# Reordering the start of each expert: preparation pieces between the additions and the reciprocal, the root ahead of the square, the first keys and queries behind the last variance

## The reference, cut to what matters

```python
def _expert(x, p):
    h = _ln(jax.nn.relu(x @ ew1 + eb1) @ ew2 + eb2, eg, ebeta)   # 128 -> 256 -> 256, layer norm: "the encoder"
    qkv = h @ aiw + aib
    q, k, v = jnp.split(qkv, 3, axis=-1)                         # 16 heads of 16
    attn = jax.nn.softmax(jnp.einsum('bhqd,bhkd->bhqk', q, k) * SCALE, axis=-1)
    ...                                                          # out projection, two LSTMs, gates, decoder
```

## Time and profile before

| | us |
|---|---|
| median of 3 runs | 4192.47 |
| lowest, highest | 4190.81, 4195.63 |
| the profiled execution | 4191.02 |
| its span in the trace | 4189.3 |

### The profile page before, as it was taken

How to read it: one execution, slowest core, us unless ns; L and a number is a source line. 1 busy time by engine, 2 the same in 40 slices (tenths; PEclk the granted TensorE clock), 3 DMA queues, 4 the chain that set the end, 5 groups by cost and what they waited for, 6 DMA issues and landing times. The chain is left out here.

```text
span 4189.3 us, 98294 instructions
## 1 busy us (share of the span) xinstructions
PE 3695.9 (88%) x36068; PEld 2265.2 (54%) x36068; DVE 2841.8 (68%) x5015; ACT 2150.3 (51%) x4378; POOL 1278.5 (31%) x1076
## 2 busy tenths in 40 slices
PE   5869689979988998952999999999999959999998
PEld 4645346646655655631555555555555527666665
DVE  8966568858858857876666666666666664555555
ACT  4536437737746755755444444444444445555554
POOL 0027537627726736744000000000000003444443
PEclk8889899989999999975999999999999978999999
DMA  8910100010010011025111111111111131111111
GB/s 174 176 33 0 52 18 2 1 56 2 0 42 16 0 42 32 0 87 157 46 50 48 45 48 50 48 44 48 49 49 43 49 103 52 54 53 53 53 53 30
DMA packets 392895, 205.07 MB, mean 49 GB/s; under 512 B 151221, under 2 KB 386474, under 8 KB 392106
## 3 DMA queue, kind: packets, MB, share of 16 engines
q1 hardware_dynamic: 392354, 203.09, 18.9%
q10 hardware_dynamic: 392, 0.03, 0.0%
HBM read 145.55 MB, written 57.51 MB: 48 GB/s over the span
## 5 line engine op out<-in xcount | busy, mean ns | idle before, releaser
L1827 PE MATMUL banks<-l_w,l_xs 128*64 128x512 f16 x6240 | 722.3, 381 | 15.0 <-DVE l_xs L1875 14.2
L1827 PE MATMUL banks<-l_w,l_hs 128*64 128x512 f16 x6144 | 705.8, 379 | 1.7 <-DVE l_hs L1881 1.7
L1827 PEld LDWEIGHTS banks<-l_w,l_xs 128*64 128x64 f16 x6240 | 344.6, 110 | 330.7 <-issue 25.6
L1827 PEld LDWEIGHTS banks<-l_w,l_hs 128*64 128x64 f16 x6144 | 348.3, 110 | 316.7 <-DVE l_hs L1881 2.2
L194 POOL MEMSET h_ident<- 128x128 f32 x1 | 0.2, 204 | 1444.3 <-POOLq L81 1444.3
L985 POOL TENSOR_TENSOR ax_p<-ax_p,ax_ri 128x520 f32<-128x520 f32 (+1 forms) x256 | 320.0, 1251 | 267.4 <-DVE ax_ri L1185 267.4
L1932 DVE SCALAR_TENSOR_TENSOR l_gates<-banks,l_unscale,l_bias 128x1024 f32<-128x1024 f32 x260 | 333.8, 1284 | 96.1 <-PE banks L1827 94.7
L1988 ACT ACTIVATE l_gates<-l_gates 128x768 f32<-128x768 f32 x260 | 219.1, 843 | 347.4 <-DVE l_gates L1932 347.4
L2259 PE MATMUL banks<-h_mem,h_w 128*128 128x320 f16 x2496 | 357.9, 300 | 1.0 <-DMA h_mem<-mem_scratch 1.0
L2554 ACT ACTIVATE h_work<-banks,h_bias,h_factor 128x320 f32<-128x320 f32 x312 | 192.3, 616 | 262.8 <-PE banks L2259 259.1
L2259 PEld LDWEIGHTS banks<-h_mem,h_w 128*128 128x128 f16 x2496 | 244.4, 98 | 94.9 <-issue 1.6
(11 more groups left out here) (306 smaller groups left out, 7180.4 us busy)
## 6 DMA issues: line engine op xcount, KB each, us to landing
image<-in_x_dram SPq DMA_DIRECT2D x192, 196.0 KB
l_x<-x_scratch SPq DMA_DIRECT2D x130, 256.0 KB, 3.0
mem_scratch<-l_hs SPq DMA_DIRECT2D x520, 64.0 KB, 1.9
h_mem<-mem_scratch SPq DMA_DIRECT2D x104, 320.0 KB, 3.7
x_scratch<-x_out SPq DMA_DIRECT2D x4, 4160.0 KB, 16.4
raw_in<-in_L_ffn_attn_in_w_dram SPq DMA_DIRECT2D x4, 768.0 KB, 4.5
h_scratch<-x_out SPq DMA_DIRECT2D x1, 2080.0 KB, 6.5
z_scratch<-z SPq DMA_DIRECT2D x1, 2080.0 KB, 11.6
```

Source lines behind the costliest of these rows:

```text
L1827: mm = pe.matmul(ps[d * HALF:(d + 1) * HALF, 2 * z + n, :], lhsT, w_of[e][:, d, kk, b, n * 512:(n + 1) * 512], start=(kk == 0 and turn_ == ...
```

## The change

It reorders instructions within the encoder and the hand-over of each expert; no arithmetic is added or taken away.

- DVE: the pieces stand between additions and reciprocal, and the first four of them one step later (2 to 5, not 1 to 4). `begin_second` stands behind the last reciprocal.
- ACT: the root stands ahead of the square. The first unit's keys are kept at step 11 and not behind the class queries and values.
- PE: the products with beta stand behind step 1 (a function of their own) and not behind step 0; values, turn and share of the largest magnitude one step later; keys and queries of the first unit behind the last variance (step 11). In unit 0, PE waits for the kept class values before the next unit's keys go into the bank that they are read from.
- POOL: the first keys are masked ahead of the class queries, and before the wait for these.

```diff
@@ pool_run
+        mask_keys(base, 0, 0, base * GROUP)
         pool.wait_ge(self.first_kept, BASE + 2 * e + 1)
         mask_class(0, base * GROUP)
-        mask_keys(base, 0, 0, base * GROUP)
@@ pe_run, unit_
                 if s == 1 and self.unit_in(u, 1):
+                    if u == 0:
+                        pe.wait_ge(self.first_kept, BASE + 2 * e + 2)
@@ act_run
         act.wait_ge(self.first_kept, BASE + 2 * e + 2)
-        self.act_keys(act, ps[:, 6, :], factor, base, 0)
@@ experts_stage, tensor
+                def sum_betas():
+
                     at = VECTORS["beta"][0]
...
-                laid_steps(body, {0: sum_vectors, 2: sum_values, 3: turn_most, 4: share_most, WSTEPS: begin})
+                laid_steps(body, {0: sum_vectors, 1: sum_betas, 3: sum_values, 4: turn_most, 5: share_most, WSTEPS + 1: begin})
@@ experts_stage, vector
-                between = {1: gain_weights, 2: measure, 3: reduce_most, 4: size, 6: lambda: low_half(0),
+                between = {2: gain_weights, 3: measure, 4: reduce_most, 5: size, 6: lambda: low_half(0),
                            7: lambda: low_half(1).then_inc(w_low, 1), 8: begin_first,
-                           9: lambda: att.dve_split(dve, e * att.UNITS, 0, e * att.UNITS * GROUP), WSTEPS: begin_second}
+                           9: lambda: att.dve_split(dve, e * att.UNITS, 0, e * att.UNITS * GROUP)}
...
                                               ALU.add).then_inc(h2_kept, 1)
+                    if k in between:
+                        between[k]()
                     if live(2):
                         dve.wait_ge(rooted, BASE + at - 1)
...
-                laid_steps(body, between)
+                laid_steps(body, {})
+                begin_second()
@@ experts_stage, scalar
+                    if live(2):
+                        act.wait_ge(varied, BASE + at_ - 1)
...
+                        act.activation(sd[:, par, :], ps[:, 4, 0:WIDE], ACT.Sqrt, bias=eps[:, 0:1]).then_inc(rooted, 1)
                     if live(1):
...
                         act.activation(sq[:, 1 - par], hc[:, (slot - 1) % RING], ACT.Square).then_inc(squared, 1)
-                    if live(2):
...
-                laid_steps(body, {5: raise_weights})
+                laid_steps(body, {5: raise_weights, WSTEPS + 1: lambda: att.act_keys(act, ps[:, 6, :], factor[:, 0:1], e * att.UNITS, 0)})
```

More of the change, by code:

```diff
@@ L1645, in body @@
                                            bias=vec[:, at + m:at + m + 1]).then_inc(h1_kept, 1)
+                    if live(2):
+                        act.wait_ge(varied, BASE + at_ - 1)
+                        if live(4):
+                            act.wait_ge(inverted, BASE + at_ - 3)
+                        act.activation(sd[:, par, :], ps[:, 4, 0:WIDE], ACT.Sqrt, bias=eps[:, 0:1]).then_inc(rooted, 1)
                     if live(1):
```

## The result

The changed kernel takes 4163.38 us (median of 4 runs, 4160.95 to 4168.73), the kernel before on the same chip 4191.67 (4 runs, 4190.81 to 4195.63): ratio 0.9932, 95% interval 0.9915 to 0.995, 28.3 us less. The forecast was 4156, its range 4147 to 4174. In a later comparison the same two gave 4163.66 and 4191.3, ratio 0.9932 [0.9919, 0.9946]. The profiled execution took 4165.48 us, 25.5 less than that of before.

What follows compares the result with a forecast made beforehand. It took PE at mostly 1.2 GHz to bound the lead-in and a DVE, ACT, DVE loop the later steps. Gains of 3.8 + 31.4 + 1.6 = 36.8 us off 4191.02 gave 4154.2, as median 4156; range 4147 to 4174.

Steps and rivals of the forecast that it cites:

- Bound and loop: Encoder's later steps: the loop DVE, ACT, DVE sets 6.17 us a step; root first breaks it, leaving PE's 5.59.
- Steady steps: Encoder, step 2 to step 9: PE sets the pace, 40.5 us against 41.45 before; square, relu and `measure` hidden.
- Tail: Encoder's end, behind step 9: step 2 to POOL's last product takes 59.0 us, was 66.85; stretch wins 31.4 in all.
- Keys and queries' move: First unit's, to behind the last variance: little by itself; up to 3 us an expert returns if their cover went.
- Lead-in: Encoder steps 0 and 1: clock rises at 7.9 us, work ends at 12.7 against 14.4; 3.8 us won in all.
- the drop behind the single columns: Lead-in: single-column products at full clock may let the clock drop again; even chance, priced 0.9 us an expert.
- Hand-over: Encoder to attention: earlier key masking gains 1.1 to 1.2 us, delays class split 0.7; net 0.4, 1.6 in all.
- rival 2: Hand-over: class split waits for the whole first key masking; gain 0.1, not 0.4 us an expert; 4157 us; chance 0.10.
- The failed step: Behind each encoder: everything waits for its last `h`, so time won there moves the rest forward whole, losing none.
- Rivals 1, 3 and 4: DVE stays the pace, 4177 us (0.15); attention or LSTM waits for a load, 4192 (0.04); ACT's queue slows steps, 4225 (0.03).
- rival 1: Encoder steps: DVE stays the pace near 6 us, POOL's product reaching into the pieces' gap; 4177 us; chance 0.15.

## Why the prediction came out as it did

- **Bound and loop.** Right. The root waits for PE's variance, the reciprocal for nothing or up to 0.4 us, and PE is the pace at 5.59 us. Putting the root first does break the loop, as was said; what the prediction didn't say is that moving the pieces does it as well (step 2 to 9: 40.61 and 40.70 us). Both are needed for the tail: with either undone the main stretch is 1.3 or 3.8 to 5.0 us longer.
- **Steady steps.** 40.5 us forecast from step 2 to 9, measured 40.70. Square, relu and `measure` were hidden as said.
- **Tail.** Forecast 59.0 for the stretch, measured 59.58. Of the 0.6, 0.4 had come by the end of the last reciprocal (1238.96 + 2.75, 57.2 us behind step 2 for the forecast 56.8), 0.2 of it with the steps. The other 0.2 came with the last POOL product: 2.25 us instead of 1.95, as `begin_second` on DVE (1241.63, 0.63 us), which I had put beside it at no cost, started just ahead of it. It is 2.3 us over four experts.
- **Keys and queries' move** was called a small thing, and is: 0.87 us.
- **Lead-in.** -4.3 against -3.8. The clock rose 8.9 us behind the start and not at 7.9, so that the stretch took 13.4 and not 12.7; but the drop behind the single columns, given an even chance at 0.9 us, didn't come in any of the four. Two errors that cancel in part. That the drop can come is shown by one lead-in of the run with the root alone: there the single columns ran at full clock (526.48, 2.82 us), and the clock fell half a microsecond behind them, at 529.7, for 3.4 us, with PE busy throughout.
- **Hand-over.** -1.6 against -1.6. 1.24 gained where 1.1 was said, and 0.82 lost where 0.7 was. The Trainium skill (SBUF — State Buffer, "Who interferes with whom") was weighed as rival 2, the lock for the whole masking; the trace agrees: the split (0.27 us by itself) lasts 1.09 and ends 0.13 us behind the masking (1244.01 + 1.03). The rows that it was priced from (rows 9) are of an operation with two inputs; the one that was held has a single one. So rival 2 was the truth of the mechanism, while its price of 0.3 us an expert more was too high, for the gain was larger as well.
- **The failed step** is the sentence that everything behind an encoder moves forward whole. The encoder did; the attention lost 1.9 us in each expert, 7.7 in all, as the half clock, which begins in PE's idle time at the encoder's end, went on 7.3 us into the attention, where it had ended 1.4 to 2.0 us into it. That is what lies between 4156 and 4163. I had read the clock in the lead-in and not at the other end. The run with fillers in all three gaps shows it: clock at full speed, 1.9 us back. The other profiles agree, expert by expert: with the clock never low there, or up 0.9 to 2.0 us behind the first max reduce, the way to the last outputs took 238.8 to 238.9 us; up at 6.0 to 6.8 us, 240.1 to 240.4; up at 6.9 to 9.1 us, 240.5 to 240.8. The two experts whose last output products ran at half clock are left out. That 4163 still lies in the range is luck of its width: no term and no rival stood for this loss.
- **Rivals 1, 3 and 4** did not come: DVE's steps didn't stay near 6, no load waited, no relu was late. The overlap that rival 1 feared did come: POOL's product now starts first and takes 1.95 us instead of 2.56, and the piece beside it 1.48 instead of 0.92; but it ends with the root, so the reciprocal isn't late.

What stays open: why the half clock lasted 13.7 us in after's hand-over and 6.8 with the masking moved by a microsecond. PE's idle gap ahead of the class products was 0.8 us shorter, but that alone doesn't do it: with the masking behind the class queries the gap is as short (3.92 us) and the half clock lasted 13.7 us. There the next gap, ahead of the class scores, is 3.21 us and not 1.98. Nothing here separates the gaps' lengths from their moments. Nor is it settled whether the wide products would pay as much without the wait of POOL; the two were run together only.

## What to carry to other kernels

Look for the operation that stands behind one it doesn't need, on both sides of a loop between two engines: a short piece between the additions and a reciprocal that waits anyway cost nothing here, while behind the reciprocal, where POOL's product starts, it could cost a multiple of itself (the split 2.30 us for 0.69). When an idle gap of PE moves, read the granted clock up to the next place where PE is waited for, as the low stretch moves too and may land on work with no slack. Where such gaps are a few microseconds long, filling them with unread wide products is a cheap trial.

## What the runs showed of the hardware

- With the 5.26 us of single-column products behind step 0 the clock was up 11.5 us or more behind the start, with step 1's wide ones there 8.9 to 9.4, though PE was busy with either but for 0.8 us. All 5.26 us ran at a granted 0.50.
- Eleven unread products of 384 columns an expert (a row of x6 is three of them in two halves each, 2.20 us) held the granted clock at 1.00 through three gaps, and took the time from 0.9915 to 0.9881 of before's. The Trainium skill (TensorE: Matmul & The Clock Gate, "What's actually happening") has the clock follow how busy PE has lately been; the trace agrees, as the half clock was gone in each gap that was filled; the single-column products above, with PE busy and the clock low, don't show it.
- A DVE operation with one input in SBUF, 128 columns of f32 to f16, was held by a POOL operation that started 0.07 us ahead of it: 1.09 us instead of 0.27, in all four experts, and 0.27 again when the POOL operation came later.
- With `begin_second` started 0.16 us ahead of it, a POOL product of 1.95 us took 2.25. Which of the two is longer went by which started first: with the piece 0.17 us ahead (1236.22, before) DVE took 0.92 us and POOL 2.56; with POOL ahead (1217.69, after) DVE took 1.48 and POOL 1.95.
